# Three step buffers in a graph attention kernel: compares three units ahead, masks two, the s1 rows spread inside the negative sums

## What is computed

```python
h  = einsum('bnf,hfo->bhno', x, W)
s1 = einsum('bhno,ho->bhn', h, a1); s2 = einsum('bhno,ho->bhn', h, a2)
e  = leaky_relu(s1[..., :, None] + s2[..., None, :], 0.2)
attn = softmax(where(adj > 0, e, -9e15), axis=-1)
x = layernorm(x + concat_heads(einsum('bhnm,bhmo->bhno', attn, h)))
```

## Time and profile before

| | |
|---|---|
| median of 3 runs | 2871.23 us (2862.51 to 2875.33) |
| the profiled execution | 2872.58 us, its span 2870.6 us |
| mean granted clock of TensorE | 0.978 |
| busy: PE / PE weight loads / DVE / ACT / POOL | 93% / 81% / 87% / 81% / 38% |
| matmuls of the positive sums, line 530 | 1019.4 us busy |
| matmuls of the negative sums, lines 561 and 562 | 1039.1 and 1038.7 us, overlapping |
| compares on ACT, line 607 | 2092.7 us |
| masks on DVE, lines 825 and 832 | 633.0 and 583.8 us |
| projection on PE, line 499 | 461.7 us |

### The profile page before, as it was taken

One profiled execution on the slowest core, in us unless ns is written; L12 is line 12 of the kernel. 1 busy time (PEld: TensorE's weight loads), 2 busy tenths in 40 slices (PEclk: granted clock), 3 DMA queues, 4 the chain that ended last, 5 costly groups with the idle time before them and its releaser, 6 DMA issues.

```text
span 2870.6 us, 126143 instructions
## 1 busy us (share of the span) xinstructions
PE 2669.8 (93%) x52546; PEld 2317.7 (81%) x52546; DVE 2510.0 (87%) x3828; ACT 2337.4 (81%) x3894; POOL 1077.6 (38%) x1011
## 2 busy tenths in 40 slices
PE   6999999999999899999999999899998999899996
PEld 3699867988589895898949998499984998759986
DVE  6898978999789988899888998889988999889996
ACT  3699974999669994799938998399983999839995
POOL 4633335333343324433253332633326233263332
PEclk9999999999999999999999999999999999999998
DMA  6467652676527754377543775447744577445773
GB/s 177 119 132 175 150 141 72 142 173 143 142 65 165 175 137 117 72 177 169 136 104 87 176 164 128 118 93 174 165 120 120 111 173 150 124 105 126 175 150 99
DMA packets 281206, 390.20 MB, mean 136 GB/s; under 512 B 161857, under 2 KB 161857, under 8 KB 280673
## 3 DMA queue, kind: packets, MB, share of 16 engines
q1 hardware_dynamic: 253536, 315.24, 41.4%
q0 software_dynamic: 27136, 67.12, 15.0%
HBM read 313.52 MB, written 34.14 MB: 121 GB/s over the span
## 4 chain that ended last, share of the span: by engine, by line
ACT 36%; PE 28%; DVE 16%; issue 13%; DMA 3%; POOL 1%; DVEq 0%; ACTq 0%; SPq 0%; POOLq 0%
ACT m_pos L607 33%; PE ps L530 10%; PE ps L499 5%; PE ps L561 5%; PE ps L562 5%; DMA y<-in_x 3%; DVE m_neg L832 3%; ACT adj_cut L573 2%; DVE m_pos L825 2%; DVE prod L796 2%; ACT xT L579 1%; DVE prod_d L799 1%; DVE m_pos L811 1%; DVE b_both L794 1%; PE ps L435 1%
## 5 line engine op out<-in xcount | busy, mean ns | idle before, releaser
L607 ACT ACTIVATE m_pos<-ps,s_steep 128x512 fp8e4<-128x512 f32 x3440 | 2092.7, 1068 | 354.0 <-PE ps L449 302.8
L530 PE MATMUL ps<-b_both,m_pos 128*128 128x130 f16 x16384 | 1019.4, 221 | 80.3 <-DVE total L670 52.0
L561 PE MATMUL ps<-d_hi,m_neg 128*128 128x65 f16 x16384 | 1039.1, 194 | 20.6 <-issue 20.2
L562 PE MATMUL ps<-d_lo,m_neg 128*128 128x65 f16 x16384 | 1038.7, 194 | 7.1 <-issue 6.7
L562 PEld LDWEIGHTS ps<-d_lo,m_neg 128*128 128x128 fp8e5 x16384 | 1010.3, 98 | 38.8 <-issue 25.4
L530 PEld LDWEIGHTS ps<-b_both,m_pos 128*128 128x128 fp8e5 x16384 | 964.2, 98 | 92.5 <-issue 91.4
L561 PEld LDWEIGHTS ps<-d_hi,m_neg 128*128 128x128 fp8e5 x16384 | 1019.7, 98 | 17.6 <-issue 17.2
L825 DVE TENSOR_TENSOR m_pos<-m_pos,maskT 128x1024 uint32<-128x1024 uint32 x512 | 633.0, 1255 | 156.1 <-ACT m_pos L607 140.0
L991 POOL TENSOR_TENSOR den_scaled<-den_inv,bound 128x4 f32<-128x4 f32 x256 | 251.3, 982 | 1260.5 <-DVE den_inv L681 1204.0
L832 DVE TENSOR_TENSOR m_neg<-m_pos,maskT 128x2048 uint32<-128x2048 uint32 x256 | 583.8, 2280 | 0.3
L499 PE MATMUL ps<-W_sb,xT 128*128 128x512 f32 x1024 | 461.7, 612 | 45.3 <-DVE prod_d L799 43.4
(11 more groups left out here) (94 smaller groups left out, 1552.3 us busy)
## 6 DMA issues: line engine op xcount, KB each, us to landing
adj_in<-in_adj SPq DMA_DIRECT2D x266, 512.0 KB, 4.8
s_bc<-s_rows SPq DMA_DIRECT2D x258, 256.0 KB, 3.6
x_in<-in_x SPq DMA_DIRECT2D x134, 256.0 KB, 4.1
x_sum<-in_x POOLq DMA_DIRECT2D x128, 256.0 KB, 4.8
y<-in_x POOLq DMA_DIRECT2D x32, 1024.0 KB, 11.0
out<-y SPq DMA_DIRECT2D x32, 1024.0 KB, 7.4
maskT<-adj_cut SPq DMA_TRANSPOSE x264, 3.9
m_neg<-in_x SPq DMA_DIRECT2D x10, 256.0 KB, 3.7
```

The lines of the kernel that those rows point to most:

```text
L530: mm = pe.matmul(acc, mask, b_both[:, j, h, :, :], start=(j == 0 and it % 2 == 0), stop=(j == JC - 1 and it % 2 == 1))
L561: pe.matmul(acc, mask, d_hi[:, j, h, :], start=(j == 0), stop=False)
L562: mm = pe.matmul(acc, mask, d_lo[:, j, h, :], start=False, stop=(j == JC - 1))
L607: ins = nc.scalar.activation(chunk(m_pos[h % 2], j, 0, BLK), ps[:, BANK_S1 + h % 2, :], ACT.Relu, bias=s2_steep[:, j, h:h + 1], scale=STEE ...
```

## The change

`m_pos` gets a third buffer, and unit u uses buffer u mod 3; `m_neg` keeps two. A compare waits for the unit that had its buffer last, three units back (`before()` gives the distance where the batch turns: 2 for units 0 and 1, 5 for unit 2). The spread of s1 for u + 3 moves into the middle of the negative sum of u, where two of its four row tiles are done; that of unit 2 goes into the projection at chunk 8; those of the next batch's units 0 and 1 stay two units ahead. DVE's iteration u becomes `make_neg(u + 1)`, the maximum of x, `take_pos(u)`, statistics, layer norm (now h = 2, 3, 4), `make_pos(u + 2)` twice, compare(u + 3), `take_neg(u)`. During the projection DVE compares unit 2 at chunk 9, where `make_neg(1)` stood, and `make_neg(1)` moves to iteration 0. SP loads s1 rows three units ahead (in the first batch that of unit 2 behind the adjacency pieces of iteration 0) and stores y at h = 6. ACT copies the next s1 in the last unit. The diff, with most of its context left out:

```diff
...
-        k, h = divmod((unit - 2) % UNITS, H)
-        if unit in (0, 1) or k * H + h == STAT_UNIT:
+        k, h = divmod((unit - 3) % UNITS, H)
+        if unit in (0, 1, 2) or k * H + h == STAT_UNIT:
             return DVE_SLOTS[1]
-        if (k and h in (2, 3)) or k * H + h in (0, STAT_UNIT + 1):
+        if k and h in (3, 4):
             return DVE_SLOTS[2]
         return DVE_SLOTS[3]
+    def before(unit):
+        return {0: UNITS - (UNITS - 2), 1: UNITS + 1 - (UNITS - 1), 2: UNITS + 2 - (UNITS - 3)}.get(unit, 3)
...
-        m_pos = [sb(f"m_pos{i}", [P, JC // 2, 2 * BLK], FP8) for i in range(2)]
+        m_pos = [sb(f"m_pos{i}", [P, JC // 2, 2 * BLK], FP8) for i in range(3)]
         m_neg = [sb(f"m_neg{i}", [P, JC // 2, 2 * BLK], FP8) for i in range(2)]
...
         pos_made = sem("pos_made", free=QUADS)
-        neg_made = sem("neg_made", free=1)
+        neg_made = sem("neg_made", free=3)
         pos_read = sem("pos_read", free=0)
...
         unit_done = sem("unit_done", free=1)
-        pos_summed = sem("pos_summed", free=1)
+        pos_summed = sem("pos_summed", free=3)
         total_made = sem("total_made")
...
                     sp.wait_ge(s1_stored, 16 * KB)
-                    load_s1(0, 0)
-                    load_s1(1, 1)
+                    for unit in range(2):
+                        load_s1(unit, unit)
                 turn_piece(q, q % 2, 0, q // 2)
...
                                 store_block(g - 1, 1)
-                        if unit == UNITS - 2:
+                        if unit == UNITS - 3:
                             sp.wait_ge(s1_stored, 16 * KB * (b + 2))
-                        load_s1(u + 2, h % 2)
+                        if unit == UNITS - 1:
+                            sp.sem_inc(waited[sp.engine], 1)
+                            with sp.If(b < B - 1):
+                                load_s1(u + 3, (h + 1) % 2)
+                        elif unit:
+                            load_s1(u + 3, (h + 1) % 2)
                         for t in range(JC):
...
                                 load_x(JC * (b + 1) + t, t % 2, ((b + 1) * (JC // 2) + t // 2) % (NBLK * IT // 2))
+                        if unit == 0:
+                            with sp.If(b < 1):
+                                load_s1(2, 0)
+                            load_s1(u + 3, (h + 1) % 2)
                         if unit == STURN_UNIT + 1:
                             store_s1(b + 1)
-                        if h == 5:
+                        if h == 6:
                             if k:
...
-            def spread_s1(unit):
+            def spread_s1(unit, u):
+                if type(u) is not int:
+                    pe.wait_ge(step_act, at(step_act, QUADS * (u - 1)))
+                    pe.sem_inc(waited[pe.engine], 1)
...
             for unit in range(2):
-                spread_s1(unit)
+                spread_s1(unit, unit)
...
                         pe.wait_ge(s1_T_copied, b + 1)
+                    if jc == 8:
+                        spread_s1(2, b * UNITS + 2)
                     if jc == 1:
...
                                         pe.sem_inc(waited[pe.engine], 1)
-                                    mask = chunk(m_pos[hp], j, it * P, P).bitcast(FP8_WIDE)
+                                    mask = chunk(m_pos[unit % 3], j, it * P, P).bitcast(FP8_WIDE)
...
                             pe.wait_ge(lo_made, at(lo_made, 2 * JC * (b + 1)))
-                        if unit == UNITS - 2:
-                            pe.wait_ge(s1_T_copied, b + 2)
-                        spread_s1((unit + 2) % UNITS)
                         if unit == STAT_UNIT + 1:
...
                         for it in range(IT):
+                            if it == IT // 2 and unit < UNITS - 3:
+                                spread_s1(unit + 3, u + 3)
+                            if it == IT // 2 and unit >= UNITS - 2:
+                                if unit == UNITS - 2:
+                                    pe.wait_ge(s1_T_copied, b + 2)
+                                spread_s1(unit + 2 - UNITS, u + 2)
                             acc = ps[:, 2 + hp, it * O1:(it + 1) * O1]
...
-            def compare(u, h, unit):
+            def compare(u, unit):
+                h = unit % H
                 act.wait_ge(s1_spread, u + 1)
...
-                act.wait_ge(neg_made, at(neg_made, u - 1))
+                act.wait_ge(neg_made, at(neg_made, u - before(unit) + 1))
                 act.sem_inc(waited[act.engine], 1)
-                act.wait_ge(pos_summed, at(pos_summed, u - 1))
+                act.wait_ge(pos_summed, at(pos_summed, u - before(unit) + 1))
                 act.sem_inc(waited[act.engine], 1)
...
                             j = qd * JQ + c
-                            ins = nc.scalar.activation(chunk(m_pos[h % 2], j, 0, BLK), ps[:, BANK_S1 + h % 2, :], ACT.Relu,
+                            ins = nc.scalar.activation(chunk(m_pos[unit % 3], j, 0, BLK), ps[:, BANK_S1 + unit % 2, :], ACT.Relu,
                                                        bias=s2_steep[:, j, h:h + 1], scale=STEEP, saturate=False)
...
             act.wait_ge(s2_turned, 1)
-            compare(0, 0, 0)
+            compare(0, 0)
...
                             copy_scores(b + 1)
-                        if unit == STAT_UNIT + 2:
+                        if unit < UNITS - 1:
+                            compare(u + 1, unit + 1)
+                        else:
                             copy_s1(b + 1)
-                        if unit < UNITS - 1:
-                            compare(u + 1, (h + 1) % H, unit + 1)
-                        else:
                             exponentials(b + 1)
...
                                 act.sem_inc(waited[act.engine], 1)
-                                compare(u + 1, 0, 0)
+                                compare(u + 1, 0)
                         for i in late:
...
-            def compare(u, h, nth, unit):
+            def compare(u, unit, nth):
+                h = unit % H
                 hp = h % 2
-                dve.wait_ge(neg_made, at(neg_made, u - 1))
+                dve.wait_ge(neg_made, at(neg_made, u - before(unit) + 1))
                 dve.sem_inc(waited[dve.engine], 1)
...
                         j = qd * JQ + c
-                        ins = V.tensor_scalar(chunk(m_pos[hp], j, 0, BLK).bitcast(FP8_WIDE), s1_bc[hp][:], s2_neg[:, j, h:h + 1],
+                        ins = V.tensor_scalar(chunk(m_pos[unit % 3], j, 0, BLK).bitcast(FP8_WIDE), s1_bc[hp][:], s2_neg[:, j, h:h + 1],
                                               STEP_UP, ALU.is_gt, ALU.mult, saturate=False)
...
-            def make_pos(u, h, mask, qd, first_of_block=None):
-                hp = h % 2
+            def make_pos(u, unit, qd, blk):
+                mask = maskT[unit // H % 2]
                 if qd == 0:
-                    if first_of_block is not None:
+                    if unit % H == 0:
                         for slot in range(2):
-                            dve.wait_ge(piece_turned[slot], at(piece_turned[slot], 16 * IT * (first_of_block + 1)))
+                            dve.wait_ge(piece_turned[slot], at(piece_turned[slot], 16 * IT * (blk + 1)))
                             dve.sem_inc(waited[dve.engine], 1)
...
                 js = slice(qd * JQ // 2, (qd + 1) * JQ // 2)
-                V.tensor_tensor(words(m_pos[hp][:, js, :]), words(m_pos[hp][:, js, :]),
+                V.tensor_tensor(words(m_pos[unit % 3][:, js, :]), words(m_pos[unit % 3][:, js, :]),
                                 words(mask[:, js, :]), ALU.bitwise_and).then_inc(pos_made, 1)
-            def make_neg(u, h, mask):
-                hp = h % 2
+            def make_neg(u, unit):
+                mask = maskT[unit // H % 2]
                 dve.wait_ge(unit_done, at(unit_done, u - 1))
                 dve.wait_ge(pos_made, at(pos_made, QUADS * (u + 1)))
-                V.tensor_tensor(words(m_neg[hp][:]), words(m_pos[hp][:]), words(mask[:]), ALU.bitwise_xor
+                V.tensor_tensor(words(m_neg[unit % 2][:]), words(m_pos[unit % 3][:]), words(mask[:]), ALU.bitwise_xor
                                 ).then_inc(neg_made, 1)
-            def make_masks(u, h, mask, first_of_block=None, before=None):
-                for qd in range(QUADS):
-                    make_pos(u, h, mask, qd, first_of_block)
-                if before is not None:
-                    take_pos(u - 1, before)
-                make_neg(u, h, mask)
...
                         with dve.If(b < 1):
-                            compare(0, 0, 0, 0)
-                            make_masks(0, 0, maskT[0], 0)
+                            compare(0, 0, 0)
+                            for qd in range(QUADS):
+                                make_pos(0, 0, qd, 0)
+                            make_neg(0, 0)
                     if jc == 6:
-                        compare(b * UNITS + 1, 1, b * (UNITS // 2), 1)
```

(37 more changed lines are left out.)

## The result

The changed kernel takes 2842.35 us (median of 9 runs, 2837.21 to 2854.55) against 2867.1 us of the kernel before beside it: a ratio of 0.9923 [0.9908, 0.9937], 0.8% faster where 3% was forecast. The profiled execution took 2844.84 us, its span is 2843.1: 27.5 less than before, where the sum had 88.5. The time lies outside the forecast's own range, 2745 to 2832.

The account below looks back on a forecast made before the run. The prediction took ScalarE to bound units 8 to 23, and waits in the chain between engines to lengthen each batch turn. Its sum was 2872.6 - 62 - 7 - 24 - 4 + 8.5 = 2784 us; own range 2745 to 2832, wide range 2735 to 2850.

Parts of the forecast that it names:

- the normalisation: Units 25 to 30: layer norm a unit later avoids 0.5 a batch lost to the residual's DMA; gain 4 us.
- Part 1: Turn to the next batch: earlier s2_neg and first split shorten TensorE's wait; gain 62 us in seven turns.
- Part 2: End of the projection and unit 0: moving make_neg(1) gains 1 us a turn, 7 us; bounds 0 and 3.5 a turn.
- d_lo term: Unit 0: the last d_lo, beside make_neg(1), takes 3.10 us, giving TensorE a new wait of 1.7.
- b_lo term: Unit 0's positive sum: VectorE's last split comes earlier, so the wait for b_lo shrinks from 2.23 to 0.4 us.
- Part 3: Units 8 to 23: ScalarE starts earlier, VectorE's new order gives part back; gain 3 a batch, 24 us.
- +6.6: Units 6 to 23: from compare(24)'s end to S(24), the start of unit 24's positive sum, 6.6 us.
- Part 4: First batch: unit 2's s1 row arrives late behind the adjacency pieces; loss about 8.5 us, once; bounds 4 and 13.
- B: Rival: the turn isn't shortened, as another condition holds the first split; 2846 us, chance 0.14.
- D: Rival: slower, as VectorE's order holds take_neg, make_neg and take_pos behind a late compare; 2920 us, chance 0.07.
- C: Rival: the lead hides all, units 6 to 23 at TensorE's own time; 2709 us, chance 0.10.
- E: Rival: the third buffer does nothing, ScalarE waits for the spread or s1 row; 2877 us, chance 0.05.

Follow-up runs that it names:

- e5_less: Changed kernel without the counter increments behind TensorE's new wait in each spread inside the loop; 2837.70 us, ratio 0.9912.
- e11_turn_less: Changed kernel without the counter increments behind TensorE's new wait and with turn_s2 earlier, behind unit 31's masks; 2804.00 us, ratio 0.9811.
- e12_all: Changed kernel with those increments removed, turn_s2 earlier, unit 2's s1 row loaded first, make_neg(1) back at chunk 9, layer norm earlier in the projection; 2775.85 us, ratio 0.9699.
- e1_pad128: Changed kernel with 128 nops ahead of TensorE's loop, which were dropped in compilation, so a repeat of it; 2839.39 us, ratio 0.9904.
- e7: Changed kernel with one ScalarE compare chunk left out in each of units 8 to 23 (result partly wrong); 2819.52 us.
- e9: Changed kernel with ScalarE's compare(u) waiting again for unit u-2's positive sum, so the third buffer gives no lead; 3057.19 us, ratio 1.0684.
- e10_turn: Changed kernel with turn_s2 moved earlier, behind unit 31's masks in iteration 29; 2841.32 us, ratio 0.9923.
- e4_ln_alone: Kernel before with only the layer norm, GpSimd's deviation and the store of y one unit later; 2852.89 us, ratio 0.9956.
- e2_row2: Changed kernel with unit 2's s1 row loaded ahead of the adjacency pieces in the first batch; 2828.29 us, ratio 0.9863.

## Why the prediction was right or wrong

Of 88.5 us of span 27.5 came. Three steps failed: the turn (26 us short), unit 0 (17 short, with the sign wrong) and the gain in units 6 to 23 (16 short). One term was too small, the normalisation, and one right.

**Part 1, half of it.** Right: S(31) comes earlier, and from s2_neg to the first split it took 16.9 us (forecast 17.0). The wait for the split does fall under 1 us, but only because an issue wait stands before it. Wrong, first, in the step "its last mask holds VectorE to 1779.7": that is S(30)+1.0, and the masks ended at S(30)+2.9. ScalarE's compare(31) was itself done at S(30)+0.7, not -0.2; and the statistics of iteration 29 (`exponents`, some 1.1 us up to 1769.03) stand before the masks, so that both halves follow in one piece, 2.36. With 0.89 of `take_pos(30)` waiting for GpSimd's y, s2_neg came 2.3 late, and the split 11.0 behind the end of unit 31's sums instead of 8.8. That alone would have left TensorE 3.16 of wait where 1.1 were forecast (e5_less). Wrong, second, in what the sum left out: the 2.8 us of fetching the loop's code. It was not there before (0.1 at most); the loop had grown by 60 instructions, and without the 32 increments among them, "the added counters", costed at nothing, it is gone. It didn't add to the first, it lay over it. Third, "after so short a wait I assume no fall of the clock": with the issue wait the gap is 2.6 to 3.8 us, and the clock fell in five turns of seven, 1.7 us each. 63.8 became 59.6 a turn, 4.1 instead of 7.8; with both causes gone it is 55.4 (e11_turn_less), where the forecast's own 55.0 of passes stood.

**Part 2, wrong in sign.** +10.4 where -7 was forecast. The d_lo term was right as a bound: 3.10 beside `make_neg(1)`, a wait of up to 1.70 against 1.7, but 1.1 on the mean. (By the Trainium skill's page "SBUF — State Buffer", section "SBUF: two separate sides", this is the exclusive port pair; VectorE started first, 1847.70 against 1847.86, as expected.) The b_lo term was mis-sized: "its last split ends 2.8 us behind TensorE's last chunk" subtracts the removed 2.2 in full. VectorE was not late throughout: at chunks 10 and 11 of every turn it waits for TensorE, 0.46 and 0.95, and there 1.4 of the 1.8 freed vanished. The lag is made afterwards, by some 6 us of layer norm in chunks 11 to 15. The wait was 1.93, not 0.4. Behind the two waits the clock was low for 6.8 us in four of these seven units (14.1 to 14.3 us each), where it was 3.4 in all seven before; the forecast named 12.2 with a fall of the clock and had nothing for a longer one. e12_all moved the lag itself and won the 3.5.

**Part 3, a third of it.** The lead came as computed: compare(8) starts at S(6)-1.4 (forecast -1.9), and ScalarE runs to the end of compare(24) in 151.8 (151.1). Its worth was mis-sized in the term "+6.6", the lag from the end of compare(24) to S(24): it measured 8.2 on the mean of the batches, so that S(24)-S(6) is 158.5, not 155.8. The 6.6 was the least lag that the new order allows, and as that it was right (6.7 is the least found in units 8 to 30). But it was set against the old kernel's actual lag, 4.0, whose own least is 2.3: TensorE stood 1.8 above the least before and stands 1.5 above it now, and the sum took the new one to stand at its least.

Between S(6) and S(24), all batches, TensorE is idle for 74.9 us before and 66.0 after. By what ended the idle time: `take_pos` 44.8 and 18.9, a mask 0 and 3.2, issue 30.1 and 43.9; the low clock lasted 20.5 and 30.7. This division is not a property of the program: the same TensorE program in e1_pad128 has 24.8, 13.8, 29.1 and 23.9. What repeats is the sum, 65 to 75 us in every run but e7 and e9. So in these two profiles the waits for `take_pos` fell by 20 and 26 us (in e10_turn, unchanged in these units, only to 39.2), and only 7 and 9 of that left the idle time; the rest came back as waits for masks, which means ScalarE, or for code. The forecast's bound of 9.7 for TensorE's own time allowed 3 us a batch of issue waits, where 3.6 to 5.7 came in the runs that keep the lead, and the clock nothing. e7 shows that this bound lies close below ScalarE's; which of the two holds a given batch I can't say from these runs.

**The normalisation was undersized.** Forecast at 4 us; units 25 to 29 gave 9.9, and in the kernel before alone it gives 14 in medians and 22 in spans (e4_ln_alone). The sentence "in these units they are already in the 159.5" was an argument for no gain in units 6 to 23, and it was backwards: a wait that is in the old number is one that can go from it (6 us in e4, where kernels alike in these units differ by up to 6.5).

**Part 4, right.** +8.7 against +8.5; e2_row2 shows the cause. The row landed at 105.7 (forecast 107) and split 10 began at 106.2 (107.4). The forecast's own rows gave 7.75 for that split, not 8.5; the other kernels with this load order start unit 0 between 118.7 and 121.4, so that it agrees to 0.2 us is luck.

**The rivals.** B (turn unchanged, 2846) came nearest in its number, but the turn did shorten by half of what was forecast, and part 2 lost 10.4 of its 29.0. That the time lies inside the wide range, 2735 to 2850, is luck: its upper end was there for B's sake. D (VectorE's order) did not happen, and e9_no_lead shows how near it was: without the lead its mechanism costs 6.8%, far more than the 2920 it was priced at, for it acts in every cycle. C (the lead hides all) did not happen either: TensorE still waits for `take_pos` in units 6 to 23. E fell, as the lead is there.

## What to carry to other kernels

A wait that is removed uncovers what ran beside it: before summing a gain, ask for each removed wait what else is due in the same microseconds, a fetch of code at a loop's end among them; when two edits each give nothing, try them together. In a ring of buffers the latency from "ready" to "start" is paid once a cycle, so an order that lengthens it must be priced against the cycle (sum, compare, lag), not once a stage. Taking work out of an engine's queue helps only behind its last idle time: look for the last wait of that engine before the point that counts, and move what stands after it. Before explaining how waits of one kind turned into another, profile the same program twice: the sum repeats better than its parts.

## What the runs showed of the hardware

- A TensorE loop waits up to 3.8 us for code at its back edge, 20.9 us in seven turns, and 32 instructions less in a loop of 13494 bring that to 1.3. The kernel before, with 13434, had 0.1 a turn at most.
- Inside the units 47 of 50 issue waits over 0.25 us, of up to 4.9, stand at the same remainder (155 to 166) of the instruction's number divided by 256, the size of a fetch: short matmuls, some 30 ns apart, do not hide the fetches.
- A GpSimd instruction on 4 columns goes from 982 to 1979 ns on the mean when VectorE's neighbouring instruction is one of 2.3 us instead of 1.2, and takes 0.2 where no mask runs beside it.
- A gap of 2.55 us before the projection passes was followed by a granted clock of 0.69 over the next 3.1 us in one turn (e10_turn), one of 2.79 before the same passes by none (1.00 over that whole turn of the changed kernel): the length of the idle time alone doesn't say whether the clock falls. Behind gaps of 1.29 (e12_all) it fell in no turn. In e9_no_lead stretches of 3.4 us at the low clock follow single gaps of 2.0 to 2.9 (six in a row between 1004 and 1107 us).
